# Layer-norm moments of x in blocks, routing ranks for two chunks at a time, receptance from two scaled weight sets

## The reference, cut to what matters

```python
x = x + cross_attention(layernorm(x), ctx, ctx)        # 257 context rows per sequence, LoRA on q, k, v, o
xi = layernorm(x)
xn = ln(xi) * g1 + b1;  xx = shift(xn)                 # shift: the row before, 0 for the first of a sequence
k = (xn * mu_k + xx * (1 - mu_k)) @ Wk
v = (xn * mu_v + xx * (1 - mu_v)) @ Wv
r = sigmoid((xn * mu_r + xx * (1 - mu_r)) @ Wr)        # the receptance
xi = xi + (r * wkv_scan(k, v)) @ Wo
ei = ln(xi) * g2 + b2
top-2 of 8 experts by softmax(ei @ router_w); xi = xi + sum of the chosen experts' outputs
x = x + xi
y = layernorm(x);  x = x + shared_geglu(y) + top-1 of 8 geglu experts of y
```

## Time and profile before

| | |
|---|---|
| median of 3 runs | 969.79 us (968.96 to 971.59) |
| the profiled execution's own time | 966.43 us |
| its span | 964.7 us |
| granted TensorE clock, mean | 0.953 of full speed |
| busy: PE, weight load, DVE, ACT, POOL | 89%, 80%, 46%, 33%, 36% |

### The profile page before, as it was taken

The page is one execution under the profiler, slowest core; times in us unless marked ns, Lnnn a source line. Parts: engine busy times, 40 slices in busy tenths (PEclk is TensorE's granted clock), DMA queues, the critical chain, the costliest instruction groups (busy, mean ns, idle before and its releaser), DMA issues. The chain is left out here.

```text
span 964.7 us, 19179 instructions
## 1 busy us (share of the span) xinstructions
PE 858.3 (89%) x6306; PEld 768.6 (80%) x6306; DVE 445.0 (46%) x1253; ACT 316.3 (33%) x712; POOL 349.3 (36%) x605
## 2 busy tenths in 40 slices
PE   5899989886667999999949999968999999999994
PEld 4567766665566889999849999957999999999993
DVE  1279989888774555555523333353111111111113
ACT  1466767664542445555411111100111111111110
POOL 1445677766775355544142222211100010000006
PEclk9899999998688989999979999989999999999998
DMA  9875557534612322263121111102998988999716
GB/s 355 277 268 189 194 112 233 155 103 188 169 43 53 79 67 83 83 214 84 50 66 33 34 38 40 38 28 73 336 330 305 329 301 324 303 319 306 270 61 175
DMA packets 92096, 161.79 MB, mean 168 GB/s; under 512 B 13832, under 2 KB 71112, under 8 KB 88680
## 3 DMA queue, kind: packets, MB, share of 16 engines
q1 hardware_dynamic: 71008, 103.39, 32.2%
q10 hardware_dynamic: 12832, 37.82, 10.5%
q0 software_dynamic: 8176, 19.57, 7.9%
HBM read 146.10 MB, written 14.66 MB: 167 GB/s over the span
## 5 line engine op out<-in xcount | busy, mean ns | idle before, releaser
L1691 PEld LDWEIGHTS bank<-zT_f,we 128*128 128x128 f32 x1472 | 167.9, 192 | 1.8 <-ACT zT_f L1979 0.7
L1691 PE MATMUL bank<-zT_f,we 128*128 128x128 f32 x1472 | 168.2, 275 | 0.5 <-ACT zT_f L1979 0.5
L1708 DVE TENSOR_TENSOR hT_f<-bank,act_g 128x512 f32<-128x512 f32 x78 | 53.8, 691 | 227.6 <-PE bank L1691 208.0
L1700 ACT ACTIVATE act_g<-bank 128x512 f32<-128x512 f32 x78 | 46.6, 597 | 320.4 <-PE bank L1691 320.4
L1691 PE MATMUL bank<-zT_c,a_x 128*128 128x128 f32 x1024 | 121.4, 281 | 0.3 <-PEq L1521 0.3
L1691 PEld LDWEIGHTS bank<-zT_c,a_x 128*128 128x128 f32 x1024 | 119.2, 197 | 0.8 <-issue 0.7
L361 POOL DMA_INDIRECT arena_a<-rows_e,pick x78 | 76.0, 975 | 29.8 <-issue 29.8
L410 PE MATMUL bank<-arena_b,arena_a 128*128 128x128 f32 x624 | 81.8, 288 | 1.6 <-DVE hT L546 1.6
L1715 PE MATMUL bank<-we,hT_f 128*128 128x256 f32 x368 | 83.2, 379 | 0.0
L410 PEld LDWEIGHTS bank<-arena_b,arena_a 128*128 128x128 f32 x624 | 78.2, 204 | 2.4 <-DVE arena_b L538 2.4
L1715 PEld LDWEIGHTS bank<-we,hT_f 128*128 128x128 f32 x368 | 68.1, 190 | 8.3
(11 more groups left out here) (273 smaller groups left out, 1361.8 us busy)
## 6 DMA issues: line engine op xcount, KB each, us to landing
we<-in_W_dram SPq DMA_DIRECT2D x69, 1024.0 KB, 7.4
arena_a<-in_ctx_n_dram ACTq DMA_DIRECT2D x16, 1152.0 KB, 7.2
arena_a<-in_ctx_t_dram SPq DMA_DIRECT2D x16, 1028.0 KB, 9.0
rows_y<-arena_a ACTq DMA_DIRECT2D x39, 128.0 KB, 1.7
arena_a<-in_w_moe_dram ACTq DMA_DIRECT2D x3, 1156.0 KB, 5.3
arena_a<-in_w_moe_dram ACTq DMA_DIRECT2D x3, 1152.0 KB, 7.5
rows_f<-yr ACTq DMA_DIRECT2D x23, 128.0 KB, 6.3
rows_e<-arena_b SPq DMA_DIRECT2D x64, 32.0 KB, 4.0
```

Of the source, the lines that this page charges most:

```text
L1691: last = nc.tensor.matmul(bank[half][:, f * P:(f + 1) * P], w12[:, i, k, col0:col0 + P], zT[:, k], start=k == 0, stop=k == KD - 1)
L1700: nc.scalar.activation(act_g[:, half], bU[half][:], ACT.Gelu).then_inc(self.ac_g, 1)
L1708: nc.vector.tensor_tensor(hT[:, parity, half * HH:(half + 1) * HH].rearrange("p f t -> p (f t)"), bG[half][:], act_g[:, half], ALU.mult).t ...
```

## The change

Three parts. **Moments**: `stats0` and `rstd0` work on a whole part of x (1, 3, 4, 4, 4 chunks). Part 0 stays ahead of the loop, part 1 comes at the start of step 0, parts 2, 3 and 4 at the end of steps 2, 4 and 5 (`STATS_AT`). POOL needs four instructions for a part in place of three for a chunk. The last two parts of x are loaded in steps 2 and 3, behind the keys of the step. **Routing**: `one_hot`, `both`, `own_rank`, `sum_rank`, `slots`, `ranks` work on two chunks at once, in the odd steps; `ranks` moves behind `values` on PE, `own_rank` behind `own_value` on DVE, `largest` behind `denominator`, `attended` ahead of `moments1`. Tokens are listed one step later (two chunks at once in steps 16 and 24, none in 17). **Receptance**: DVE mixes two inputs in place of three. PE multiplies the normed rows by Wr scaled by mu_r, and the shifted rows by Wr scaled by 1 - mu_r, and adds both in PSUM: eight matmuls in place of four. The two weight sets are made once, by DVE in step 3.

```diff
-            def rstd0(n):                                   # POOL, three instructions on 128x1
...
+            def rstd0(i):
+                lo, hi = X_PARTS[i]
+                v, r, m = (rs0[:, j, lo:hi] for j in range(3))
+                pool.wait_ge(dv_st0, i + 1)
+                nc.gpsimd.tensor_scalar(v, mv0[:, lo:hi, 1], EPS, None, ALU.add).then_inc(po_v0, 1)
+                pool.wait_ge(po_v0, i + 1)
+                nc.gpsimd.tensor_tensor(r, v, eps_pow[:].to_broadcast([P, hi - lo]), ALU.pow).then_inc(po_p0, 1)
+                pool.wait_ge(po_p0, i + 1)
+                nc.gpsimd.tensor_scalar(m, mv0[:, lo:hi, 0], -1.0, None, ALU.mult).then_inc(po_n0, 1)
+                pool.wait_ge(po_n0, i + 1)
+                nc.gpsimd.tensor_tensor(m, m, r, ALU.mult).then_inc(po_r0, 1)
...
@@ POOL, the loop over the steps
-                if live(s + 1) is not None:
-                    rstd0(s + 1)
+                if s == 0:
+                    rstd0(1)
...
                 if c is not None:
                     rstd1(c)
+                if s in STATS_AT:                           # {2: 2, 4: 3, 5: 4}
+                    rstd0(STATS_AT[s])
                 if s == 1:
                     time_mix_constants()
                 if s == 2:
                     routing_constants()
...
@@ PE
             def receptance(n):
+                if n == 0:
+                    pe.wait_ge(dv_rw2, 1)
+                pe.wait_ge(ac_xn, n + 1)
                 need(pe, ac_er, n)
                 upto(ac_q, pe, n + LAG + 2)
-                product(n, 2, bQR).then_inc(pe_r, 1)
+                for m in range(KD):
+                    for k in range(KD):
+                        for h, w in enumerate((t_w[:, 2, k], r_prev[:, k])):
+                            last = nc.tensor.matmul(of_seq(bQR[:, m * P:(m + 1) * P]), w[:, m * P:(m + 1) * P],
+                                                    xn[n % 2][:, k, :, 1 - h:1 - h + S],
+                                                    start=k == 0 and h == 0, stop=k == KD - 1 and h == 1)
+                last.then_inc(pe_r, 1)
...
+            def ranks(q):
+                pe.wait_ge(dv_mask, q + 1)
+                need(pe, po_sum, 2 * q)
+                need(pe, dv_prod, q)
+                upto(dv_dk, pe, 2 * q + 6)
+                two, odd = bK[:, D:D + 2 * E], bK[:, D + E:D + 2 * E]
+                nc.tensor.matmul(two, before_m[:], mask[:].rearrange("p c e -> p (c e)"), start=True, stop=False)
+                nc.tensor.matmul(bK[:, D:D + E], ones_m[:], earlier[:, q % 2], start=False, stop=False)
+                nc.tensor.matmul(odd, ones_m[:], earlier[:, q % 2], start=False, stop=False)
+                nc.tensor.matmul(odd, ones_m[:], mask[:, 0], start=False, stop=True).then_inc(pe_rank, 1)
...
-                if h is not None:
-                    ranks(h)
                 if b is not None:
                     attended(b)
...
                     values(k)
+                if h == CUT:
+                    totals_a()
+                if h is not None and h % 2:
+                    ranks(h // 2)
+                if k is not None:
                     receptance(k)
...
@@ DVE
+            def receptance_weights():
+                nc.vector.tensor_scalar(one_mu, mu[:, 2], -1.0, 1.0, ALU.mult, ALU.add)
+                dve.drain()
+                for k in range(KD):
+                    nc.vector.tensor_scalar(r_prev[:, k], t_w[:, 2, k], one_mu[:, k:k + 1], None, ALU.mult)
+                dve.drain()
+                for k in range(KD):
+                    last = nc.vector.tensor_scalar(t_w[:, 2, k], t_w[:, 2, k], mu[:, 2, k:k + 1], None, ALU.mult)
+                last.then_inc(dv_rw2, 1)
...
             def mixed(n):
-                need(dve, pe_r, n - 1)
-                for i in range(3):
+                need(dve, pe_vv, n - 1)
+                for i in range(2):
...
@@ DVE, the loop over the steps, cut to what moves
+                if s == 0:
+                    stats0(1)
-                if t is not None:
-                    stats0(t)
...
-                if t is not None:
-                    moments0(t)
-                if h is not None:
-                    largest(h)
...
                     denominator(w)
+                if h is not None:
+                    largest(h)
...
+                if b is not None:
+                    attended(b)
                 dve.drain()
                 if c is not None:
                     moments1(c)
...
                 if a is not None:
                     own_value(a)
+                if q is not None:
+                    own_rank(q)
                 dve.drain()
+                if q is not None:
+                    sum_rank()
                 if z is not None:
                     mixed(z)
+                if z == 0:
+                    receptance_weights()
+                if q is not None:
+                    dve.drain()
+                    slots(q)
                 if h == CUT:
                     tile_map_a()
                 if a is not None:
                     largest_score(a)
+                if s in STATS_AT:
+                    stats0(STATS_AT[s])
```

More of the change, by code:

```diff
@@ L736, in mix_pool @@
                 if i is not None:
-                    list_tokens(i)
+                    for n in listed_at(i):
+                        list_tokens(n)
                 if g is not None:
                     normed(g)
-                if h is not None:
-                    count(h)
+                if h is not None and h % 2:
+                    count(h // 2)
                 if a is not None:
@@ L914, in keys @@
                 need(pe, dv_dk, n)
[L915 removed]
+                need(pe, dv_prod, (n - 4) // 2)
                 if n >= CUT + 5:
@@ L1010, in normed @@
             def normed(n):
-                act.wait_ge(po_r0, n + 1)
+                act.wait_ge(po_r0, 1 + [i for i, (lo, hi) in enumerate(X_PARTS) if lo <= n < hi][0])
                 need(act, pe_h, n - 1)
-                nc.scalar.activation(hn[:, n % 2], xz[:, n], ACT.Identity, bias=rs0[:, n % 2, 2:3],
-                                     scale=rs0[:, n % 2, 1:2]).then_inc(ac_hn, 1)
+                nc.scalar.activation(hn[:, n % 2], xz[:, n], ACT.Identity, bias=rs0[:, 2, n:n + 1],
+                                     scale=rs0[:, 1, n:n + 1]).then_inc(ac_hn, 1)
             def normed1(n):
@@ L1177, in mix_vector, with stats0 @@
         def mix_vector(dve):
-            def stats0(n):
-                part = [i for i, (lo, hi) in enumerate(X_PARTS) if lo <= n < hi][0]
-                dve.wait_ge(ld_x[part], 16)
-                nc.vector.bn_stats(st0[:, n % 2], xz[:, n])
-            def moments0(n):
-                nc.vector.bn_aggr(mv0[:, n % 2], st0[:, n % 2]).then_inc(dv_st0, 1)
+            def stats0(i):
+                lo, hi = X_PARTS[i]
+                dve.wait_ge(ld_x[i], 16)
+                for n in range(lo, hi):
+                    nc.vector.bn_stats(st0[:, n % 4], xz[:, n])
+                dve.drain()
+                for n in range(lo, hi):
+                    last = nc.vector.bn_aggr(mv0[:, n], st0[:, n % 4])
+                last.then_inc(dv_st0, 1)
             def own_value(n):
@@ L1393, in mix_vector @@
                     weight_sum(w)
-                if t is not None:
-                    moments0(t)
+                    value_sum(w)
+                dve.drain()
+                if w is not None:
+                    new_value(w)
+                    denominator(w)
                 if h is not None:
                     largest(h)
-                if w is not None:
-                    value_sum(w)
                 dve.drain()
@@ L1411, in mix_vector @@
                 dve.drain()
-                if h is not None:
-                    both(h)
+                if q is not None:
+                    one_hot(q)
                 if k is not None:
@@ L1420, in mix_vector @@
                 dve.drain()
+                if q is not None:
+                    both(q)
                 if x is not None:
@@ L1431, in mix_vector @@
                     residual_att(c)
-                if h is not None:
-                    own_rank(h)
                 dve.drain()
@@ L1441, in mix_vector @@
                     moments1(c)
-                if h is not None:
-                    slots(h)
-                if b is not None:
-                    attended(b)
                 if z is not None:
```

121 lines of the change are left out of this document (57 added, 64 removed).

## The result

The changed kernel takes **975.72 us** (median of 9 runs, 973.14 to 977.61) beside 969.79 us of the kernel before in the same session (9 runs, 968.64 to 971.59): ratio **1.0057**, 95% interval 1.0043 to 1.0071. It is 5.9 us slower; the forecast was 969.1, most likely no change.

A forecast was written before the change was run, and what follows sets the result against it. Three bounds within 2 us: a DVE-POOL-ACT ring (14.2 us a late step), DVE's work and PE's. Terms +1.3 + 4.2 + 2.5 - 4.3 - 4.4 = -0.7 gave 965.7, plus 3.4 to the median 969.1 us; range 961 to 977.

The forecast's parts named there:

- DVE's wait for the ranks: Odd steps, priced in steps 10 to 15: DVE's `own_rank` waits 1.5 us for ranks PE makes behind `values`.
- Step 0: Pipeline start: moments of part 1's three chunks stand ahead of the scores, +1.3 us (0.9 to 1.6).
- Step 3, the constants: Step 3: constants behind part 2's rstd0 make ACT's `scaled_in` 4.1 late; weight sets less mixing +1.0; +4.2 (2.5 to 5).
- that rival: PE's clock falls in the fill, where PE stands some 3 us in step 3: +4 us, 973; chance 0.05.
- Step 4: No cost of its own; 1.9 us of bn_stats and bn_aggr at its end, felt in the following step.
- Steps 5 to 9: PE takes DVE's place as bound: 65.3 us in place of 62.8, +2.5 (+1 to +5).
- Steps 10 to 15: Two steps take 27.0 us, 13.5 each; 81 us in place of 85.2, -4.3 (-7.2 to 0).
- the 2.5 that stood as a limit: Late steps: the forecast calls itself wrong if a step's waits at `own_rank` exceed 2.5 us.
- The tail: Steps 16 to 24: less mixing and routing on DVE, `largest` wait covered, -4.4 us (-6 to -1).
- Receptance: PE in each step: eight more passes cost 0.9 us, none doubled; DVE loses two mixing instructions, -0.55.
- The first rival: Steps 10 to 15: less DVE mixing relieves POOL, PE alone sets 13.0 a step; 963.7 us, chance 0.33.
- the ring: Late steps: DVE's `new_value`, POOL's row 10.9, ACT 1.9, DVE 1.4 to the next `new_value`; 14.2 us, the step.

The follow-up runs named there:

- e1: Kernel before with the moments part of the change alone; 970.60 us, ratio 1.0050 to the kernel before.
- e17: e1 with 14 matmuls whose result nothing reads in PE's wait of step 3; 977.19 us, ratio 1.0041 to the kernel before.
- e4: Changed kernel with moments of chunks 4 to 7 and their 1/sqrt at the end of step 1 instead of 2; 970.63 us, ratio 1.0047 to before.
- e8: e3 with DVE's `attended` back behind `moments1`; 967.46 us, ratio 1.0002 to the kernel before.
- e3: Kernel before with the routing part of the change alone, including its order of DVE's loop; 972.31 us, ratio 1.0056 to the kernel before.
- e14: Kernel before with DVE's `attended` ahead of `moments1` and nothing else of the change; 971.95 us, ratio 1.0072 to the kernel before.
- e9: Whole changed kernel with only DVE's `attended` back behind `moments1`; 978.07 us, ratio 1.0035 to the kernel before.
- e6: e5 with DVE's `attended` also back behind `moments1`; 966.73 us, ratio 0.9998 to the kernel before.
- e5: Changed kernel with the time mixing's first-column memsets ahead of rstd0 in step 2 and routing constants in step 3; 968.89 us, ratio 1.0016 to before.
- e11: e6 with receptance on mixed rows as before, and PE's ranks ahead of the values; 968.83 us, ratio 0.9940 to the kernel before.
- e15: e6 with PE's ranks ahead of the values; 963.49 us, ratio 0.9971 to the kernel before.
- e13: e1 with 26 matmuls whose result nothing reads in PE's wait of step 3; 975.24 us, ratio 1.0084 to the kernel before.

## Why the prediction was wrong, point by point

Most terms came out near their size. The forecast failed in three steps: it left PE's clock out of the price of its own wait in step 3, it gave step 4 no term at all, and it let DVE's wait for the ranks begin in step 10 in place of step 9.

- **Step 0**: +1.5, forecast 1.3. Right, though this stretch varies by 0.7 from kernel to kernel.
- **Step 3, the constants**: right in kind and size. ACT's `scaled_in` comes 7.38 us after the end of step 2, 3.05 before: 4.3 late, forecast 4.1; the weight sets less the saved mixing cost 0.9, forecast 1.0. The step lost 5.9, not 4.2; the difference is PE's clock, 1.5 us by the rows of the change and 2.2 in e1, shown by e17. The forecast had named that rival, with 4 us and a chance of 0.05, as a case apart, though its cause, PE standing for 3 us, was part of the forecast itself. That was the mis-set chance.
- **Step 4, the term that is missing.** Step 4 lost 1.2 and its clock was 0.85; e4, with the same code in it, has 9.6 at clock 1.00. So this is the clock again, and nothing in the working allowed for it. The diff also moves `attended` ahead of `moments1`, and the working prices neither the move nor what queues behind it. Its price is clear of the intervals in kernels without the other parts: 5.2 us (e8 against e3) and 7 (e14). In the whole change it reads 2.1 (e9) and 1.7 (e6 against e5), neither clear of them. That it cost something in the change is likely and not shown.
- **Steps 5 to 9**: PE did become the bound; from 100 to 142 us it waits once, for 0.35 us. Steps 5 to 8 took 12.89, 13.32, 12.76 and 13.01, forecast 12.8, 13.5, 12.9, 13.0. Step 9 took 15.06, forecast 13.1: it is the first odd step with ranks, and DVE waits for them there already (1.58 us), which was priced only from step 10 on. Step 10 takes 11.54, and the two together the 26.6 that the forecast gives them; but the stretch up to step 15 now has four long odd steps and three short even ones.
- **Steps 10 to 15**: 81.6, forecast 81. Right, and for the reason given: DVE waits 1.99 at `own_rank` in step 13 (forecast 1.5), and e11 shows that this wait sets the pair. In step 11 it was 2.73, over the 2.5 that stood as a limit: ACT stood 1.21 us there with no releaser of its own. The same code has 1.47 in e5, and there step 11 takes 15.1 us in place of 16.4. From step 5 to step 15 the kernel is 2.3 us over the forecast, and 1.3 of them are this one step.

```profile
193.96 0.19 DVE L1356 TENSOR_TENSOR hot_rank<-hot,bank 128x32 f32<-128x32 f32 x1 [1.99 <-PE bank L953]
```

- **The tail**: steps 16 to 19 gave 3.5, forecast 3.9 of the 4.4. The profiled execution then loses 3.5 up to the tile map, in which DVE starts 2 us after PE's totals with no releaser of its own:

```profile
312.40 0.17 PE L964 MATMUL bank<-earlier,ones_m 128*128 128x8 bf16 x1
...
314.48 0.29 DVE L1398 TENSOR_TENSOR scratch<-bank,tile_lo 128x128 f32<-128x128 f32 x1 [6.35 <-remote]
```

  The token lists don't explain that. The stretch takes 36.7 to 39.4 in the three sessions where before has a median of 967 to 968 us, and 41.9 to 43.7 in the two where it has 973 to 974, with and without the routing. The profile of before has 38.3, but its execution (966.43) is not one of the nine beside the change, which all took longer. What makes it differ wasn't tried.
- **Receptance**: passes of 0.11 each, none doubled. Right.
- **A row misread.** The first rival took GpSimd's 0.79 at 181.19 as time beside the mixing. The mixing starts at 182.35; beside the 0.79 runs `change` (L1224, from 181.18, 0.42 us), which stays. So the relief that the rival expects from two mixing instructions less can't be read from this row.

Up to the end of the stretch "16-19" the two profiles lie 6.5 us apart, near the 5.9 of the medians, where the forecast's terms sum to -0.2. The 6.7 us between are 1.7 in step 3 and 1.2 in step 4, nearly all the clock's; 2.3 in steps 5 to 15; 0.8 in step 1, no more than its spread; and a few tenths in steps 0 and 16 to 19.

## What to carry to other kernels

In the fill of a pipeline, price every reordering on an engine that idles, too: what it moves behind a wait is late for all that follow, though no busy time changes. Where PE will stand idle for a few microseconds, look at its granted clock behind such waits elsewhere in the trace and add the slow passes to the wait, not as a rival; behind a wait of about 2 us the clock fell in some kernels here and not in others, so give that a chance of its own. And when results are batched over two steps, look where the consumer waits in the batching step: there one swap on the producer brought 0.44%, most of what the best kernels win.

## What the runs showed of the hardware

- **One late microsecond can bring the clock down, and need not.** With PE's wait at `out_T` at 1.85 us in place of 0.90, the granted clock was 0.81 over 9 us of e3 and step 3 took 2.6 us more. With 1.89 and 1.87 in the same place e5 and e14 kept 1.00, and e6 and e15, with the same 2.00 us of wait in step 4, had 1.00 and 0.83.
- **`pow` on GpSimd by columns**: 0.57 us for one, 0.90 for three, 1.04 for four in step 3 of the change, and 1.49 and 1.53 for four in its steps 5 and 6, where DVE is busier.
- **The same steps settle at two lengths.** e1, e13 and e17 have the same code from step 4 on. Steps 13 to 15 take 13.4 us each in e1 and e17, 14.1 in e13. GpSimd's small two-operand instructions differ (e1, then e13):

```profile
201.30 0.27 POOL L702 TENSOR_SCALAR rs<-mv,rs 128x1 f32<-128x1 f32 x1
202.69 0.39 POOL L683 TENSOR_SCALAR rs<-mv,rs 128x1 f32<-128x1 f32 x1
203.06 0.47 POOL L684 TENSOR_SCALAR rs<-mv,rs 128x1 f32<-128x1 f32 x1
```
```profile
204.17 0.54 POOL L702 TENSOR_SCALAR rs<-mv,rs 128x1 f32<-128x1 f32 x1
205.81 0.53 POOL L683 TENSOR_SCALAR rs<-mv,rs 128x1 f32<-128x1 f32 x1
206.33 0.80 POOL L684 TENSOR_SCALAR rs<-mv,rs 128x1 f32<-128x1 f32 x1
```

  0.27 + 0.14 + 0.33 is the 0.74 us of the step, and they stand on the ring. That they set its length was seen, not tried. Which DVE instructions run beside them doesn't explain it: in both kernels `change` starts 0.07 to 0.08 us behind L702, and the mixing runs beside the other two. The Trainium skill (SBUF — State Buffer, section SBUF: two separate sides) describes a port pair for which a GpSimd instruction that reads SBUF and a DVE instruction with two SBUF inputs exclude each other; the rows don't contradict it, and no run here shows that it is the cause.
